# Two norms between two attentions, computed on tokens-major tiles inside the first attention

## The reference, cut to what matters

```python
x = _layernorm(x + _L2_attn_ref(x, w_aq, w_ak, w_av, w_ao), axis=-1)   # 8 heads of 128, causal, rope
# _L2_ffn_ref(x, ...), first lines
xn = _rmsnorm(x, gamma1)                     # x / sqrt(mean(x*x) + 1e-5) * gamma1
q = xn @ q_w + q_b ...                       # 16 heads of 64, causal, rope
attn_out = ctx @ o_w + o_b + xn
```

## Time and profile before

| | us |
|---|---|
| median of 3 runs (1771.27 to 1776.8) | 1772.24 |
| the profiled execution's own time | 1770.54 |
| its span in the trace | 1768.4 |
| TensorE busy | 1613.3 (91%) |
| VectorE busy | 1049.9 (59%) |
| ScalarE busy | 1012.7 (57%) |
| GpSimd busy | 746.8 (42%) |

### The profile page before, as it was taken

How to read it: one execution, slowest core, us unless ns; L and a number is a source line. 1 busy time by engine, 2 the same in 40 slices (tenths; PEclk the granted TensorE clock), 3 DMA queues, 4 the chain that set the end, 5 groups by cost and what they waited for, 6 DMA issues and landing times. The chain is left out here.

```text
span 1768.4 us, 28482 instructions
## 1 busy us (share of the span) xinstructions
PE 1613.3 (91%) x9207; PEld 1084.4 (61%) x9225; DVE 1049.9 (59%) x2605; ACT 1012.7 (57%) x2188; POOL 746.8 (42%) x683
## 2 busy tenths in 40 slices
PE   5888998888798899999799999999999999888998
PEld 3556754346596677777555555555458886344786
DVE  5865775623122666666366666666558886662675
ACT  4534563553243555555466666666548887754786
POOL 1234533105252566655265555555234443021463
PEclk8999998998899999999999999999989999989999
DMA  1008323000214223232211111111046562000420
GB/s 43 2 15 179 69 73 142 1 1 30 68 34 138 60 65 68 61 69 51 78 44 47 47 40 47 47 39 49 19 144 218 219 221 87 1 1 22 148 108 25
DMA packets 61868, 124.71 MB, mean 71 GB/s; under 512 B 14258, under 2 KB 29477, under 8 KB 55228
## 3 DMA queue, kind: packets, MB, share of 16 engines
q1 hardware_dynamic: 59580, 119.24, 23.1%
q0 software_dynamic: 2144, 3.70, 0.7%
HBM read 79.05 MB, written 11.02 MB: 51 GB/s over the span
## 5 line engine op out<-in xcount | busy, mean ns | idle before, releaser
L1992 ACT ACTIVATE h_probs<-psum,h_nmax 128x512 f32<-128x512 f32 (+3 forms) x256 | 133.2, 526 | 119.0 <-DVE h_nmax L2073 64.1
L2073 DVE CUSTOM_DVE_ANT_0 psum<-psum,h_mask 128x512 f32<-128x512 f32 (+3 forms) x256 | 122.6, 511 | 83.3 <-PE psum L1876 80.4
L917 ACT ACTIVATE psum<-psum,f_b 128x512 f32<-128x512 f32 x200 | 132.3, 662 | 30.0 <-PE psum L874 30.0
L1804 POOL TENSOR_TENSOR h_swapped<-h_swapped,rope_tables 128x512 f32<-128x512 f32 x64 | 81.8, 1278 | 153.6 <-DMA h_swapped<-h_raw 153.6
L840 POOL TENSOR_TENSOR e_lo<-e_gated,e_hi 128x512 fp32r<-128x512 f32 x59 | 76.0, 1289 | 150.3 <-ACT e_hi L929 150.3
L2425 ACT ACTIVATE a_probs<-psum,a_nmax 128x512 f32<-128x512 f32 (+3 forms) x128 | 67.5, 527 | 120.7 <-DVE a_nmax L2500 70.3
L2246 POOL TENSOR_TENSOR a_swapped<-a_swapped,a2f_a_tables 128x512 f32<-128x512 f32 x64 | 82.0, 1281 | 127.1 <-DMA a_swapped<-a_raw 127.0
L952 DVE TENSOR_TENSOR e_lo<-psum,e_hi 128x512 fp32r<-128x512 f32 x168 | 114.8, 683 | 24.9 <-ACT psum L917 24.9
L126 PE MATMUL psum<-rope_tables,mean_w 128*128 128x256 f32 x482 | 118.3, 396 | 7.0 <-ACT h_raw L1982 2.8
L1883 PEld LDWEIGHTS psum<-ident,h_probs 128*128 128x128 f32 x640 | 71.4, 141 | 80.4 <-issue 52.8
L1883 PE MATMUL psum<-ident,h_probs 128*128 128x128 f32 x640 | 115.1, 287 | 1.7 <-ACT h_probs L1992 1.4
(11 more groups left out here) (501 smaller groups left out, 4135.7 us busy)
## 6 DMA issues: line engine op xcount, KB each, us to landing
e_gate<-gates SPq DMA_DIRECT2D x39, 1024.0 KB, 4.7
a_swapped<-a_raw SPq DMA_DIRECT2D x128, 128.0 KB, 2.3
h_swapped<-h_raw SPq DMA_DIRECT2D x256, 64.0 KB, 2.0
e_gate<-gates SPq DMA_DIRECT2D x16, 512.0 KB, 8.0
f_w<-in_l_experts SPq DMA_DIRECT2D x32, 128.0 KB, 4.6
slots<-a_empty SPq DMA_DIRECT2D x1, 2600.0 KB
f_w<-in_l_experts SPq DMA_DIRECT2D x9, 256.0 KB, 4.9
e_got<-slots SPq DMA_DIRECT2D x7, 325.0 KB, 4.2
```

Source lines behind the costliest of these rows:

```text
L917: nc.scalar.activation(to, hidden_bank(n), ex.act_func, **bias(n)).then_inc(act_ready, 1)
L1992: nc.scalar.activation(probs[:, j % 4, 0:(q + 1) * P], ring[j % RING][:, 0:(q + 1) * P], ACT.Exp, scale=-1.0, bias=nmax[:, j % 8:j % 8 + 1 ...
L2073: nc.vector.tensor_tensor_reduce(s, s, mask[:, (QT - 1 - q) * P:], scale=-1.0, scalar=-SENT, op0=ALU.add, op1=ALU.min, accum_out=nmax[:, j ...
```

## The change

The layernorm and the RMS norm of a batch are computed inside `token_attention`, on the running sum with tokens on partitions, by the new class `TokenNorm`. The batch's moments come from VectorE (`bn_stats` on each of four 128x128 tiles, then `bn_aggr`), at n = 0 of the unit with U % G == 1. ScalarE makes both inverse roots from the variance alone with two logarithms and one exponential on 128x4 and 128x8 elements (after a layernorm the mean square is var / (var + 1e-5), so the second norm's factor follows from it; that is the new constant 1e-10 in `c_eps`). VectorE scales the four tiles twice with a `tensor_scalar` of two scalars per partition: k = 0 for x at n = 3 of the same unit, k = 1 for xn at n = 0 of the next. TensorE turns them back in the units with U % G == 2 and 3, at n = 2, into `misc[1]`; VectorE copies the first to `core.x`, ScalarE copies the second times gamma1 to `xn`, both at n = 3, and `project_k` of those units waits for them. `turn_back` and `sum_out` go. For the last batch the same steps stand at the end, with `keep_busy` of 20 instead of 8 ahead of the transposes. `total` now lies in `core.sum`. Stage "h2" gets `Ready` for its head: no norms and no table load there. Its weight loads (`following.sync`) are issued by SyncE in the first attention, once, behind the swaps of unit 8.

```diff
+class TokenNorm:
+    def __init__(self, core, st, name, gamma, plain, scaled):
...
+    def moments(self, dve, b, tokens):
+        if b >= 1:
+            dve.wait_ge(self.scaled_ready, 2 * b)
+            dve.wait_ge(self.logs_ready, 2 * b)
+        for t in range(QT):
+            last = self.nc.vector.bn_stats(self.stats[:, t, :], tokens[:, t, :])
+        last.then_inc(self.measured, 1)
+        dve.wait_ge(self.measured, b + 1)
+        for t in range(QT):
+            last = self.nc.vector.bn_aggr(self.mean_var[:, t, :], self.stats[:, t, :])
+        last.then_inc(self.gathered, 1)
+    def invert(self, act, b):
+        act.wait_ge(self.gathered, b + 1)
+        if b >= 1:
+            act.wait_ge(self.scaled_ready, 2 * b)
+        var = self.mean_var[:, :, 1]
+        self.nc.scalar.activation(self.inverse[:, 0, :], var, ACT.Ln, bias=self.core.eps[:, 0:1]).then_inc(self.logs_ready, 1)
+        self.nc.scalar.activation(self.inverse[:, 1, :], var, ACT.Ln, scale=1.0 + 1e-5, bias=self.core.eps[:, 3:4]).then_inc(self.logs_ready, 1)
+        act.wait_ge(self.logs_ready, 2 * b + 2)
+        self.nc.scalar.activation(self.inverse[:], self.inverse[:], ACT.Exp, scale=-0.5).then_inc(self.inverse_ready, 1)
+    def scale(self, dve, b, k, tokens):
+        dve.wait_ge(self.inverse_ready, b + 1)
+        if b >= 1:
+            dve.wait_ge(self.turned, 2 * (b - 1) + k + 1)
+        for t in range(QT):
+            last = self.nc.vector.tensor_scalar(self.out[:, k, t, :], tokens[:, t, :], self.mean_var[:, t, 0:1], self.inverse[:, k, t:t + 1],
+                                                ALU.subtract, ALU.mult)
+        last.then_inc(self.scaled_ready, 1)
+    def turn(self, pe, b, k, bank):
+        pe.wait_ge(self.scaled_ready, 2 * b + k + 1)
+        for t in range(QT):
+            last = self.nc.tensor.transpose(bank[:, t * P:(t + 1) * P], self.out[:, k, t, :], self.core.ident[:])
+        last.then_inc(self.turned, 1)
+    def copy_plain(self, dve, b, bank):
+        dve.wait_ge(self.turned, 2 * b + 1)
+        self.nc.vector.tensor_copy(self.plain[:, cols(b)], bank).then_inc(self.plain_out, 1)
+    def copy_scaled(self, act, b, bank):
+        act.wait_ge(self.turned, 2 * b + 2)
+        self.nc.scalar.activation(self.scaled[:, cols(b)], bank, ACT.Copy, scale=self.gamma).then_inc(self.scaled_out, 1)
...
-        total = st.sb("total", [P, B, QT, P])
+        total = core.sum[:].rearrange("p (b t d) -> p b t d", b=B, t=QT)
...
+                    if V == G:
+                        following.sync(sp)
...
-                    if V - AHEAD > G:
-                        pe.wait_ge(sum_done, (V - AHEAD - 1) // G)
+                    U = V - AHEAD
+                    if U - 3 >= G:
+                        pe.wait_ge(norm.scaled_out, (U - 3) // G)
+                    if U - 2 >= G:
+                        pe.wait_ge(norm.plain_out, (U - 2) // G)
...
-                def turn_back(b):
-                    pe.wait_ge(added, G * (b + 1))
-                    if b + 1 < B:
-                        pe.wait_ge(raw_ready[1], G * (b + 1) + 1 + AHEAD)
-                    for t in range(QT):
-                        last = nc.tensor.transpose(misc[1][:, t * P:(t + 1) * P], total[:, b, t, :], core.ident[:])
-                    last.then_inc(turned, 1)
...
-                        if U > 1 and U % G == 1:
-                            turn_back(U // G - 1)
+                        for k in range(2):
+                            if U > G and U % G == 2 + k:
+                                pe.wait_ge(raw_ready[1], U + AHEAD)
+                                norm.turn(pe, U // G - 1, k, misc[1])
...
-                keep_busy(core, pe, 0, 8)
-                turn_back(B - 1)
+                keep_busy(core, pe, 0, 20)
+                for k in range(2):
+                    norm.turn(pe, B - 1, k, misc[k])
                 keep_busy(core, pe, 0, 3)
...
+                    if n == 2 and U > G and U % G == 1:
+                        norm.invert(act, U // G - 1)
+                    if n == 3 and U > G and U % G == 3:
+                        norm.copy_scaled(act, U // G - 1, misc[1])
+                norm.invert(act, B - 1)
+                norm.copy_scaled(act, B - 1, misc[1])
...
-                def sum_out(b):
-                    dve.wait_ge(turned, b + 1)
-                    nc.vector.tensor_copy(core.sum[:, cols(b)], misc[1]).then_inc(sum_done, 1)
...
-                    if n == 3 and U > 1 and U % G == 1:
-                        sum_out(U // G - 1)
+                    if U > G and U % G == 1 and n == 0:
+                        dve.wait_ge(added, G * (U // G))
+                        norm.moments(dve, U // G - 1, total[:, U // G - 1, :, :])
+                    if U > G and U % G == 1 and n == 3:
+                        norm.scale(dve, U // G - 1, 0, total[:, U // G - 1, :, :])
+                    if U > G and U % G == 2 and n == 0:
+                        norm.scale(dve, U // G - 1, 1, total[:, U // G - 1, :, :])
+                    if U > G and U % G == 2 and n == 3:
+                        norm.copy_plain(dve, U // G - 1, misc[1])
                 inverse_sums(NU - 1)
                 normalise(NU - 1)
-                sum_out(B - 1)
+                dve.wait_ge(added, NU)
+                norm.moments(dve, B - 1, total[:, B - 1, :, :])
+                for k in range(2):
+                    norm.scale(dve, B - 1, k, total[:, B - 1, :, :])
+                norm.copy_plain(dve, B - 1, misc[0])
 
 
...
-            after_a2 = layer_norm(core, sh, "n2a", xc=(5, 3, 4, 7), var=(0, 1))
-            g1 = Norm(core, sh, "g1", core.x, xn, center=False, eps_col=0, gamma=core.gammas[:, 0, 0:1], src_ready=after_a2.out_ready, var=(5, 3, 4, 7))
-            rope_attention(core, "h2", rope, Head(core, after_a2, g1, rope), x=xn, heads=2)
+            attn2(core, xn, rope)
+            recycle(core)
+            rope_attention(core, "h2", rope, Ready(Ahead()), x=xn, heads=2)
```

More of the change, by code:

```diff
@@ L2162, in _ @@
                 add_out(B - 1)
-def token_attention(core, name, front, head, *, x):
+class TokenNorm:
+    def __init__(self, core, st, name, gamma, plain, scaled):
+        self.core, self.nc, self.gamma, self.plain, self.scaled = core, core.nc, gamma, plain, scaled
+        self.stats = st.sb(f"{name}_stats", [P, QT, 6])
+        self.mean_var = st.sb(f"{name}_mean_var", [P, QT, 2])
+        self.inverse = st.sb(f"{name}_inverse", [P, 2, QT])
+        self.out = st.sb(f"{name}_out", [P, 2, QT, P])
+        self.measured, self.gathered, self.logs_ready, self.inverse_ready, self.scaled_ready, self.turned, self.plain_out, self.scaled_out = (
+            st.sem(f"{name}_{n}") for n in ("measured", "gathered", "logs_ready", "inverse_ready", "scaled_ready", "turned", "plain_out", "scaled_out"))
+    def moments(self, dve, b, tokens):
[37 more added lines that the diff above has]
+        self.nc.scalar.activation(self.scaled[:, cols(b)], bank, ACT.Copy, scale=self.gamma).then_inc(self.scaled_out, 1)
@@ L2175, in token_attention, with __init__, wait, sync @@
+class Ready:
+    def __init__(self, ahead):
+        self.ahead = ahead
+    def wait(self, engine, b):
+        pass
+    def sync(self, sp):
+        self.ahead.sync(sp)
+    def gpsimd(self, pool):
+        pass
+    def tensor(self, pe):
+        pass
+    def scalar(self, act):
+        self.ahead.scalar(act)
+    def vector(self, dve):
+        pass
+def token_attention(core, name, front, head, *, x, gamma, scaled, following):
     nc = core.nc
@@ L2219, in token_attention @@
          s_ready, max_ready, probs_ready, pt_psum, copied_dve, copied_act, rinv_ready, xw_psum, xw_ready, values_done, added,
[L2220 removed]
+         ) = (st.sem(n) for n in (
              "w_rounded", "w_split", "x_rounded", "x_split", "wvo_rounded", "wvo_split", "mask_zeroed", "mask_set", "proj_ready", "prep_psum",
              "sin_ready", "qk_ready", "s_ready", "max_ready", "probs_ready", "pt_psum", "copied_dve", "copied_act", "rinv_ready",
[L2223 removed]
+             "xw_psum", "xw_ready", "values_done", "added"))
         total_set = [st.sem(f"{n}_total_set") for n in ("even", "odd")]
+        norm = TokenNorm(core, st, "norm", gamma, x, scaled)
         ring = [core.psum[:, k, :] for k in range(RING)]
```

9 lines of the change are left out of this document (3 added, 6 removed).

## The result

The changed kernel takes 1783.02 us in the median of 12 runs (1773.7 to 1790.4), the kernel before, beside it on the same chip, 1772.24 (12 runs, 1765.64 to 1783.17). The ratio is 1.005 with a 95% interval of 1.0028 to 1.0072: slower by 8.9 us, with 5.0 and 12.8 as ends. The forecast was 1777.9 us, 0.32% above before; by the ratio the kernel stands at 1781.1, within the range, by its own median 0.5 us beyond its upper end, 1782.5.

A forecast was written before the change was run, and what follows sets the result against it. TensorE was taken to bound the first attention, the chain of norms the stage handover. Three batches at +4.8 us (+14.4) less 8.75 gave +5.65: 1776.2 us against the profiled execution, 1777.9 against the median; range 1770.5 to 1782.5.

The forecast's parts named there:

- The handover between the stages: Between first attention and second stage: norm passes go, `keep_busy` ends last, first projection 8.75 us earlier (bounds 7.5 to 9.5).
- rival (d): Stage handover shortened by less, through a table load or a weight in flight: +1.3 us; no separate chance, within the bounds.
- `moments`: VectorE in unit U % G == 1, ahead of step 2's maximum: 1.45 us against 0.60 slack, stopping TensorE 0.85 us.
- `scale(0)` held by GpSimd: Unit U % G == 1: `scale(0)` waits for GpSimd's addition; unit 2.2 us longer including `moments`, 0.85 without the meeting.
- rival (a): VectorE and GpSimd do not stop each other for a `tensor_scalar`: 3.46 us per batch, 1773.9 us in all; chance 0.28.
- `scale(1)`: VectorE in unit U % G == 2, ahead of step 2's maximum: 0.86 us, over the 0.60 slack by 0.26.
- The turning back: Units U % G == 2 and 3: transposes plus `project_k` waiting for VectorE's, then ScalarE's copy: 1.24 and 2.35 us.
- what would show it: Signs in the later profile, among them handover units of about 10.3, 9.6 and 10.4 us against 8.06 to 8.08 plain.
- The loads: Weight loads behind unit 8's swap in the first attention: next swap 1 to 2 us late, cost 0, bound above 3.
- if the swap of unit 9 stops TensorE: First attention, the swap behind the weight loads: a listed sign that the prediction is wrong.
- rival (c): `moments` takes 1.6 us or more, second cosine meets GpSimd, loads cost 2 to 3: about 1782 us; chance 0.14.
- Everything behind the first projection is as before: Second stage after its first projection: no change in time, so 0 in the sum.

The follow-up runs named there:

- dve_moved: Changed kernel with `moments` at step 3 of units U % G == 0 and both `scale` at step 1 of units U % G == 2 and 3; ratio 0.9997.
- scale0_moved: Changed kernel with `scale(0)` at n = 1 of the next unit and `scale(1)` at n = 0 of the one after; 1776.77 us beside 1775.03.
- turn_early: Changed kernel with the transposes at n = 1 instead of 2 and both copies at n = 2, VectorE's ahead of its `normalise`; ratio 1.0012.
- late_loads: Changed kernel with the ten loads back at the start of the second stage; ratio 1.0054.
- spread_loads: Changed kernel with the ten loads issued one per unit, behind the swaps of units 9 to 18; ratio 1.0027.
- kb13: Changed kernel with `keep_busy` of 13 instead of 20 ahead of the last batch's transposes; ratio 1.002.
- stream_same: kb13 with the seven `keep_busy` it lacks put in at the first attention's start; 1783.85 us beside 1775.03.
- all_best: Changed kernel with spread_loads, dve_moved, kb13 and turn_early (one unit later) together; 1761.39 us beside 1771.88 for the kernel before, ratio 0.995.

## Why the prediction was right, and where it was off

**Bound.** TensorE without idle time, the chain of norms between the stages: both held. In the attention every wait put in front of TensorE came out in the length of a unit; between the stages TensorE's added `keep_busy` ended last, as worked out, though 3.05 us behind the chain it covers where the prediction had 1.2 (856.56 less 855.4).

**The handover between the stages.** -8.75 predicted, -8.83 measured. The table load of rival (d) did not come; the barrier took 1.65 us (1.61).

**`moments`.** 1.45 predicted, 1.25 measured with its wait (669.33 to 670.58); behind the slack 0.85 predicted, 0.48 measured.

**`scale(0)` held by GpSimd.** This decided between the forecast and rival (a), and it is shown: 0.83 and 1.43 us beside 0.34, 2.70 for the four beside 1.08, and gone in dve_moved and in scale0_moved, where the same four stand at a step without GpSimd. That first unit's 2.2 us of the prediction is, in the trace, 0.48 and 1.5 of the 1.60. The Trainium skill, page "SBUF — State Buffer", section "SBUF: two separate sides", has the shared port exclusive for an instruction's whole length; the runs agree for a `tensor_scalar` with two scalars per partition, which ends 0.07 to 0.09 us after GpSimd's. Rival (a), 3.46 per batch, is refuted; measured are 4.46.

**`scale(1)`.** 0.26 predicted; what is left for it in the 2.07 is 0.1. It is 1.08 us long, not 0.86: with two scalars per partition an instruction of 128x128 takes 0.34 us. In this place that was hidden.

**The turning back.** 1.24 and 2.35 predicted, 1.25 and 2.38 measured. `project_k` waits 0.57 us for VectorE and 1.69 for ScalarE (about 1.6 predicted). turn_early shows that this was avoidable.

Per batch +4.8 was predicted and +4.46 measured; three times, 14.4 against 13.4. The excess falls on four intervals of `normalise` and not on three, as "what would show it" had it, since `moments` stands ahead of one `normalise` and `scale(0)` behind it.

**The loads.** This step failed, and "if the swap of unit 9 stops TensorE" was one of the prediction's own signs of being wrong. The prediction had SyncE free in time, which held, and the swap "1 to 2 us late", priced at 0. It landed 3.4 us late and cost 3.46 us, beyond the bound of 3. The row it leaned on, GpSimd late by 4.64 us at no cost, was right, but the slack ended soon behind it: 6.33 us already cost 1.8. What was missing is that the ten loads are in flight together when the swap is issued, so that it shares the engines with all of their bytes, and that a stall can bring the clock down behind it. late_loads and spread_loads show the size; over the eight kernels that load in a burst it was 1.75 to 3.7. The loads' part of rival (c) came true; its other part, a cosine that meets GpSimd because of `moments`, did not.

**A term not in the sum.** "Everything behind the first projection is as before" was wrong by 1.87 us: the first swap lands 1.6 us late, 0.97 of it by one long issue. kb13 and stream_same show with what it comes and goes.

So 5.65 less 1.04 for the batches, plus 3.46 for the loads, plus 1.87 for the swap, less 0.08 at the handover is 9.86, the difference in the traces.

That the time still fell within the range is in part luck. The two terms that the sum held at nothing came to 5.3 us, nearly as much as the whole forecast of 5.65, and only the 1 us that the batches cost less, and a range drawn for part of rival (c), kept the time inside: 1781.1 is nearer to (c)'s 1782 than to the forecast's 1777.9. The handover of a batch and the one between the stages were right by their mechanism.

## What to carry to other kernels

Before VectorE work is put into a gap, look at what GpSimd does at that moment: the same four instructions cost 1.5 us per batch at one step and nothing at another. A free step is free only while GpSimd keeps its time: in one handover of scale0_moved and one of all_best a `tensor_scalar` met it all the same. A copy that frees the bank of the next product belongs as early as its data allow, on the engine whose queue is empty then. Loads for a later stage go one at a time behind transfers that are waited for, not in one burst; and the filler ahead of a handover should be as long as the chain it covers, not longer.

## What the runs showed of the hardware that was not expected

- A VectorE `tensor_scalar` on 128x128 with one SBUF tensor and two scalars per partition takes 0.34 us alone; beside a GpSimd instruction it ends 0.07 to 0.09 us after that one, up to 1.43 us in all. The cosine with two SBUF inputs ended 0.54 us after it, by the earlier trace rows.
- `bn_stats` on four tiles of 128x128 takes 0.84 us, `bn_aggr` on their four results 0.38.
- DMA issues by SyncE took 1.07 to 2.12 us instead of 0.59 where a packet of instructions arrived at the same time: four of a swap in the kernel before and five in the changed one. Seven `keep_busy` fewer on TensorE moved the packet and removed the long issue behind the first projection; seven put in elsewhere brought both back.
- After a stretch in which TensorE was busy 3.58 of 5 us the granted clock was 0.68 over the next 5 us, and it cost about 1.6 us; after a deeper one in kb13, busy 1.38 of 3 us, it stayed at 1.00.
- Ten loads issued in a row, eight of them of 257 KB, made the swap behind them land 5.8 to 7.8 us after its issue at its slowest, against 2.3 undisturbed and 4.1 at the slowest in the kernel before.
